# A conditioned residual chain on one core: who issues the first mix weights and the last stores, and the attention table made in four row tiles

## The chip, the cores and the metric

One core of a Trainium2 chip runs the kernel. The metric is the device time of one execution in microseconds (us), the median of several runs.

## The reference

Four residual layers work on x, 32 samples of 128 channels by 2048 positions, all float32. Layers 0 and 3 are grouped convolutions of 9 taps in 4 groups; layers 1 and 2 mix the channels with a matrix that is a softmax-weighted sum of 8 matrices, a different one for every sample.

```python
x = x + conv(x, w0, groups=4, pad=4) + (cond @ c_w0.T)[:, :, None] + side[None, :, None]
for L in (1, 2):
    h   = gelu(gelu(cond @ W0 + b0) @ W1 + b1)
    att = softmax(h @ W2 + b2)                       # 32 x 8
    x   = x + einsum('boi,bih->boh', einsum('bk,koi->boi', att, weight), x) + (att @ bias_k)[:, :, None]
x = x + conv(x, w3, groups=4, pad=4) + (cond @ c_w3.T)[:, :, None] + side[None, :, None]
```

## The kernel before, in words

The positions of a sample are dealt into 4 phases (PH), so that a group of 32 channels times 4 phases fills 128 rows. Every fp32 operand is split into a high and a low part (`x_hi`, `x_lo`, `taps_hi`, ...), and a convolution is 36 turns (TURNS): 12 shifts times three products (high by high, low weights by high, high by low). One turn is four matmuls on four row tiles of 32 rows (`conv_turns`, L836). The two mix layers are one: TensorE multiplies the two matrices of a sample (`product`, L886 and L893), VectorE splits the product into `prod` (`split_product`), four DMAs spread it over the row groups of `mix_w` (`spread_mix_w`, L326), and 48 matmuls apply it (`mix`, L906).

Per sample the order on TensorE is conv0, half of the conv3 of the sample before, product of the next sample, the rest of that conv3, mix. ScalarE makes the high parts (`high_y`, `high_z`, `high_x`), VectorE the low parts (`low_y`, `low_z`, `low_x`) and the sums of 8 matrices (`mix_matrices`, L669, 16 instructions a sample). SyncE issues the loads, the relays, the stores and the spreading of `mix_w`. Engines run in program order and wait on semaphores.

**The start** is written out by hand in each engine's block. TensorE: dummy matmuls (`keep_busy`), the transposes of cond and of the small rows, `hidden(0)`, then the 36 turns of conv0 of sample 0 with the small work put between them: `hidden(1)`, `logits`, the transposes of the context weights, `mix2_transposes(0)`, `contexts`, two transposes of the attention, the matmul that spreads the attention over all rows into the table `att_tab` (L1030), `mix2_transposes(1)`, `conv_biases`, the bias through the mix (`mixed_bias`, 10 matmuls, L955), and after 25 turns `product(zero, 0)`. After turn 36 come 16 turns of conv0 of sample 1, then `mix(zero)`, which waits for `y_lo_done` (the four low parts of y of sample 0, L630) and `mix_w_spread` (the four DMAs, L326, which wait for `prod_lo_done`). VectorE makes the softmax, `att_tab`, the low parts of x, the matrices, the split of the product, 8 more matrix steps, and `low_y(zero)`. ScalarE makes the high taps, the gelus, the exponentials, the planes of sample 1, and then `high_y(zero)` (L465).

**The end.** SyncE's queue stores sample 31 in eight pieces of 128 KB (half h, group g; L378) and between the first four and the last four the two halves of sample 30 (512 KB each, L371), which ScalarE weaves (`weave_half`, L542). The first half's pieces wait for VectorE, the second half's for ScalarE's bias (`bias_last`, L533), which follows VectorE's transposes (L728, L731).

```python
for h in range(2):
    if h == 1:
        for part in range(2):
            sp.wait_ge(halves_woven, part + 1)
            ...
    for g in ((2, 3, 0, 1), range(G))[h]:
        ...
```

Of the kernel before, what the change touches and what calls it, by code (L numbers as in the profile page):

```python
# [24 lines left out]
F32 = mybir.dt.float32  # L25
# [6 lines left out]
G = 4  # L32
# [6 lines left out]
K = 8  # L39
# [7 lines left out]
MIXED = K + 2  # L47
# [3 lines left out]
def conditioned_residual_kernel(nc, x, cond, side, conv0_w, ctx0_w, mix1, mix2, conv3_w, ctx3_w, out):  # L51
# [9 lines left out]
    with ctx:  # L61
# [35 lines left out]
        ones = sb("ones", [GC, C])  # L97
# [17 lines left out]
        key_w = [o1[:, 1544 + K * l:1544 + K * l + K] for l in range(2)]  # L115
        key_b = [o1[0:1, 1560 + K * l:1560 + K * l + K] for l in range(2)]
        bias_k = [o1[0:K, 1576 + 128 * l:1704 + 128 * l] for l in range(2)]
        hid = [[o1[:, 1832 + 32 * (2 * l + m):1864 + 32 * (2 * l + m)] for m in range(2)] for l in range(2)]
# [4 lines left out]
        soft = sb("soft", [N, 64])  # L123
        att_exp = [soft[:, K * l:K * l + K] for l in range(2)]
        att = [soft[:, 16 + K * l:16 + K * l + K] for l in range(2)]
        att_max = [soft[:, 32 + l:33 + l] for l in range(2)]
        att_sum = [soft[:, 34 + l:35 + l] for l in range(2)]
        att_inv = [soft[:, 36 + l:37 + l] for l in range(2)]
        attT_sb = sb("attT_sb", [K, 2, N])
        spread = sb("spread", [N, N, 2 * K])  # L130
# [9 lines left out]
        key_w_in = sem("key_w_in")  # L140
        key_b_in = sem("key_b_in")
# [12 lines left out]
        condT_done = sem("condT_done")  # L154
        ctxT_psum = sem("ctxT_psum")
# [12 lines left out]
        att_step = sem("att_step")  # L168
        spread_done = sem("spread_done")
        attT_psum = sem("attT_psum")  # L170
# [127 lines left out]
        def _(sp):  # L298
# [21 lines left out]
            def spread_mix_w(t, d):  # L320
# [36 lines left out]
            spread_mix_w(zero, 0)  # L357
# [8 lines left out]
            for h in range(2):  # L366
                if h == 1:
                    for part in range(2):
                        sp.wait_ge(halves_woven, part + 1)
                        run = slice(part * L // 2, (part + 1) * L // 2)  # L370
                        sp.dma_start(out[N - 2, :, run].rearrange("(g o) x -> o g x", g=G), out_sb[0][:, run])\  # L371
                          .then_inc(out_stored[0], DMA)
                for g in ((2, 3, 0, 1), range(G))[h]:
                    if h == 0 and g >= 2:
                        sp.wait_ge(last_runs[h], g + 1)
                    else:
                        sp.wait_ge(last_biased[h], g + 1)
                    sp.dma_start(out[N - 1, rows(g), h * L // 2:(h + 1) * L // 2].rearrange("o (i x) -> o i x", i=RUNS),  # L378
                                 last_out[:, h, g, :]).then_inc(out_stored[1], DMA)
# [4 lines left out]
        def _(pool):  # L384
# [48 lines left out]
            for n, m in enumerate((mix1, mix2)):  # L433
                pool.dma_start(key_w[n], m[4]).then_inc(key_w_in, DMA)
                pool.dma_start(key_b[n], m[5].rearrange("(a k) -> a k", a=1)).then_inc(key_b_in, DMA)
            for l, m in enumerate((mix1, mix2)):
                pool.dma_start(bias_k[l], m[7]).then_inc(bias_k_in, DMA)
# [7 lines left out]
        def _(act):  # L445
# [45 lines left out]

            def gelus(m):
                act.wait_ge(hidden_psum, m + 1)
                for l in range(2):
                    act.activation(hid[l][m], ps[:, 6, 64 + 32 * (2 * m + l):96 + 32 * (2 * m + l)], ACT.Gelu,
                                   bias=mlp_b[l][m]).then_inc(hidden_done, 1)
# [47 lines left out]

            def product_out(t, d):
# [547 lines left out]
```

## Time and profile before

| | us |
|---|---|
| median of 3 runs | 663.0 (662.95 to 663.0) |
| the profiled execution's own time | 663.23 |
| its span, first to last instruction | 661.4 |
| TensorE busy | 650.6 |
| last matmul ends | 652.84 |
| `mix(zero)` starts | 31.29 |

The profile covers one execution, with times from the start of its span. A timeline row gives start, duration, engine, line, operation, output and inputs, and in brackets how long the engine was idle before it and what ended that. SPq and ACTq are DMA issues in the instruction streams of SyncE and ScalarE. The chain of waits is the work that ended last, followed back from the end. A matmul row of "x2" can be one fp32 matmul, which shows as two passes.

### The profile page before, as it was taken

How to read it: one execution, taken by the hardware profiler on the slowest of the kernel's cores; microseconds unless marked ns; L12 is line 12 of the kernel's file. 1: busy time of each engine (PE TensorE's matmuls, PEld its weight loads, DVE VectorE, ACT ScalarE, POOL GpSimd, SP SyncE). 2: the span in 40 equal slices, each digit the busy share in tenths (PEclk: the TensorE clock that was granted, in tenths of full speed). 3: DMA queues.
4: the chain of work that ended last, by engine and by line, in shares of the span. 5: the costliest groups of instructions: out<-in, count | busy, mean ns of one | idle time of the engine just before them, and what ended most of it. 6: DMA issues, size and time to landing. Idle time of an engine off the chain costs nothing.

```text
span 661.4 us, 24661 instructions
## 1 busy us (share of the span) xinstructions
PE 650.6 (98%) x11220; PEld 595.9 (90%) x11220; DVE 476.5 (72%) x945; ACT 262.3 (40%) x328; POOL 241.7 (37%) x85
## 2 busy tenths in 40 slices
PE   8999999999999999999999999999999999999994
PEld 6889999999999999999999999999999999999994
DVE  7898867687767677677677677677677677677635
ACT  4643424433424433424433423433423433433434
POOL 3024334433424433434443433442433442433220
PEclk9999999999999999999999999999999999999998
DMA  7355776454566455566455566545566545444515
GB/s 235 97 162 161 224 224 213 155 175 183 168 222 219 153 168 191 159 222 222 156 163 194 154 222 222 165 153 199 150 223 223 164 154 205 153 154 161 159 67 192
DMA packets 50325, 118.77 MB, mean 180 GB/s; under 512 B 5557, under 2 KB 26090, under 8 KB 42474
## 3 DMA queue, kind: packets, MB, share of 16 engines
q1 hardware_dynamic: 49602, 117.48, 54.7%
q8 instruction: 28, 0.46, 0.3%
q10 hardware_dynamic: 488, 0.69, 0.3%
q14 instruction: 15, 0.12, 0.1%
q0 software_dynamic: 192, 0.02, 0.0%
HBM read 35.33 MB, written 33.55 MB: 104 GB/s over the span
## 4 chain that ended last, share of the span: by engine, by line
PE 96%; DVE 1%; DMA 1%; SPq 0%; ACTq 0%; ACT 0%; issue 0%
PE ps L836 79%; PE ps L906 14%; PE ps L893 1%; DMA out_planes<-in_L_cond_b 1%; PE ps L874 1%; DVE x_in L728 1%; DMA mix_w<-prod 1%; DVE x_planes L731 0%; PE ps L955 0%; SPq L326 0%; PE ps L943 0%; ACTq L554 0%; ACT x_planes L533 0%; PE ps L981 0%; PE ps L886 0%
## 5 line engine op out<-in xcount | busy, mean ns | idle before, releaser
L399 POOL COPY out_sb<-out_planes 128x2048 f32<-128x2048 f32 x30 | 118.7, 3956 | 220.4 <-DVE mat2T L669 208.4
L390 POOL COPY x_planes<-x_in 128x2048 f32<-128x2048 f32 x29 | 112.7, 3887 | 137.8 <-DVE x_lo L616 137.8
L465 ACT ACTIVATE y_hi<-ps,bias_tab 128x512 fp32r<-128x512 f32 x128 | 77.5, 689 | 189.1 <-PE ps L836 189.1
L640 DVE SCALAR_TENSOR_TENSOR z_lo<-ps,bias_tab,z_hi 128x1024 fp32r<-128x1024 f32 x62 | 76.8, 1280 | 69.2 <-ACT z_hi L475 69.2
L630 DVE SCALAR_TENSOR_TENSOR y_lo<-ps,bias_tab,y_hi 128x512 fp32r<-128x512 f32 x128 | 87.3, 745 | 38.9 <-ACT y_hi L465 38.9
L836 PE MATMUL ps<-z_hi,taps_lo 32*128 32x512 f32 x1488 | 99.4, 397 | 0.0
L836 PE MATMUL ps<-x_hi,taps_hi 32*128 32x512 f32 x1536 | 97.2, 391 | 0.0
L836 PE MATMUL ps<-x_hi,taps_lo 32*128 32x512 f32 x1536 | 96.5, 389 | 0.0
L836 PE MATMUL ps<-x_lo,taps_hi 32*128 32x512 f32 x1536 | 96.0, 390 | 0.0
L836 PE MATMUL ps<-z_hi,taps_hi 32*128 32x512 f32 x1488 | 92.9, 391 | 0.0
L483 ACT ACTIVATE out_taps<-ps,bias_tab 128x512 f32<-128x512 f32 x62 | 39.3, 684 | 134.3 <-PE ps L836 134.3
L836 PE MATMUL ps<-z_lo,taps_hi 32*128 32x512 f32 x1488 | 92.5, 390 | 0.0
L906 PE MATMUL ps<-y_hi,mix_w 32*128 32x512 f32 x1024 | 89.8, 389 | 0.3 <-DMA mix_w<-prod 0.3
L836 PEld LDWEIGHTS ps<-x_hi,taps_hi 32*128 32x128 f32 x1536 | 82.4, 184 | 7.1 <-issue 0.4
L836 PEld LDWEIGHTS ps<-x_lo,taps_hi 32*128 32x128 f32 x1536 | 82.2, 183 | 7.1
L836 PEld LDWEIGHTS ps<-x_hi,taps_lo 32*128 32x128 f32 x1536 | 82.4, 183 | 6.7 <-issue 0.2
L836 PEld LDWEIGHTS ps<-z_hi,taps_hi 32*128 32x128 f32 x1488 | 79.9, 183 | 7.0
L836 PEld LDWEIGHTS ps<-z_lo,taps_hi 32*128 32x128 f32 x1488 | 80.0, 183 | 6.7
L475 ACT ACTIVATE z_hi<-ps,bias_tab 128x1024 fp32r<-128x1024 f32 x62 | 65.7, 1112 | 50.0 <-PE ps L906 50.0
L836 PEld LDWEIGHTS ps<-z_hi,taps_lo 32*128 32x128 f32 x1488 | 77.0, 184 | 5.7
L616 DVE TENSOR_TENSOR x_lo<-x_planes,x_hi 128x2048 fp32r<-128x2048 f32 x31 | 70.8, 2284 | 0.0
L650 DVE TENSOR_SCALAR out_taps<-ps,bias_tab 128x512 f32<-128x512 f32 x62 | 43.7, 747 | 23.2 <-PE ps L836 23.2
(122 smaller groups left out, 554.2 us busy)
## 6 DMA issues: line engine op xcount, KB each, us to landing
x_in<-in_x SPq DMA_DIRECT2D x31, 1024.0 KB, 5.2
out_planes<-out_taps SPq DMA_DIRECT2D x122, 256.0 KB, 2.5
out<-out_sb SPq DMA_DIRECT2D x30, 1024.0 KB, 4.5
mix_w<-prod SPq DMA_DIRECT2D x128, 128.0 KB, 3.6
x_in<-in_x SPq DMA_DIRECT2D x2, 512.0 KB, 5.4
out<-x_planes SPq DMA_DIRECT2D x8, 128.0 KB, 2.1
out<-out_sb SPq DMA_DIRECT2D x2, 512.0 KB, 3.5
out_taps<-in_L_cond_weight SPq DMA_DIRECT2D x1, 512.0 KB, 6.5
```

The lines of the kernel that those rows point to most:

```text
L390: pool.tensor_copy(x_planes[:, :, :], planes(x_in[t.par(d)], slice(0, S))).then_inc(x_planed, 1)
L399: pool.tensor_copy(out_sb[t.par(d)][:, :].rearrange("c (s p) -> c p s", p=PH), out_planes[:, :, :])\
L465: act.activation(y_hi[:, g, :], ps[:, bank(t, 0) + g, :], ACT.Identity, bias=bias_tab[:, b, g:g + 1]).then_inc(y_hi_done, 1)
L475: act.activation(z_home(t, 0)[0][:, 2 * h:2 * h + 2, 1:S + 1], ps[:, k:k + 2, :], ACT.Identity, bias=bias_tab[:, b, 2 * G:BIAS]).then_inc( ...
L483: act.activation(out_taps[:, g, :], ps[:, bank(t, d) + g, :], ACT.Identity, bias=bias_tab[:, b, G + g:G + g + 1]).then_inc(out_act, 1)
L616: dve.tensor_tensor(out=x_lo[p][:, :, 1:S + 1], in0=x_planes[:, :, :], in1=x_hi[p][:, :, 1:S + 1].bitcast(F32), op=ALU.subtract).then_inc( ...
L630: dve.scalar_tensor_tensor(out=y_lo[:, g, :], in0=ps[:, bank(t, 0) + g, :], scalar=bias_tab[:, b, g:g + 1], in1=y_hi[:, g, :].bitcast(F32) ...
L640: dve.scalar_tensor_tensor(out=z_home(t, 0)[1][:, 2 * h:2 * h + 2, 1:S + 1], in0=ps[:, k:k + 2, :], scalar=bias_tab[:, b, 2 * G:BIAS], in1 ...
L650: dve.tensor_scalar(out_taps[:, g, :], ps[:, bank(t, d) + g, :], bias_tab[:, b, G + g:G + g + 1], None, ALU.add).then_inc(out_dve, 1)
L728: dve.transpose(blocks(last_mid[:, h, g, :]), taps).then_inc(last_turned[h], 1)
L836: tile = pe.matmul(ps[:, first_bank + g, :], w[rows(g), d, :], a[rows(g), d % PH, d // PH:d // PH + S], start=(n == 0), stop=(n == TURNS - 1))
L906: tile = pe.matmul(ps[:, bank(t, 0) + p, :], w[rows(p), g, h, :], a[rows(p), g, :], start=(n == 0), stop=(n == 3 * G - 1))
```

## The change

- **End**: the first half of sample 30 is stored by SyncE after two of the eight pieces of sample 31; the second half is issued by ScalarE (`store_woven`), between its weave and `bias_last`. SyncE issues nine stores instead of ten.
- **First mix weights**: of the four DMAs that spread `mix_w` of sample 0, SyncE issues two and ScalarE two (`spread_first`), ahead of `high_y(zero)`. One of ScalarE's four `taps_high(1, p)` moves behind `high_y(zero)`.
- **Attention**: `hid` of the second layer is stored four times side by side (128 columns), so the logits come out on 128 rows, the same 32 samples in each of four row groups; both softmaxes run as one set of instructions; each row group keeps its own 8 samples (`own_samples`), and four matmuls of 32 rows by 128 columns, on four row tiles, make the table instead of one of 32 rows by 512. The transposed attention comes from a VectorE transpose of 32x32, and both layers' keys for the bias are one operand of 16 rows, so `mixed_bias` has 9 matmuls instead of 10.
- **Order of the start**: `hidden(0)` stands ahead of the wait for the small rows; `contexts` and `conv_biases` move back; `product(zero, 0)` comes after 34 turns instead of 25; 18 turns of conv0 of sample 1 stand ahead of `mix(zero)` instead of 16. On VectorE the low parts of x come in single phases and mostly behind the table; on ScalarE both `plane_x1` come behind `agg`.

The diff, cut:

```diff
-MIXED = K + 2
+MIXED = K + 1
+SAMPLES = N // G
...
             zero = Step(0, 0)
-            spread_mix_w(zero, 0)
+            spread_mix_w(zero, 0, range(2))
...
             relay_out(ALL[N], -2, range(2))
-            for h in range(2):
-                if h == 1:
-                    for part in range(2):
-                        sp.wait_ge(halves_woven, part + 1)
...
+            store_group(0, 2)
+            store_group(0, 3)
+            sp.wait_ge(halves_woven, 1)
+            sp.dma_start(out[N - 2, :, 0:L // 2].rearrange("(g o) x -> o g x", g=G), out_sb[0][:, 0:L // 2])\
+              .then_inc(out_stored[0], DMA)
+            store_group(0, 0)
+            store_group(0, 1)
+            for g in range(G):
+                store_group(1, g)
...
+            def spread_first():
+                act.wait_ge(prod_hi_done, 1)
+                act.wait_ge(prod_lo_done, 1)
+                for p in range(2, PH):
+                    act.dma_start(mix_w[0][rows(p), :, :, :].rearrange("o g h z -> o g (h z)").bitcast(F32),
+                                  prod[:, :, :].rearrange("m h z -> m (h z)").bitcast(F32))\
+                       .then_inc(mix_w_spread[0], DMA)
...
+            def store_woven():
+                act.wait_ge(halves_woven, 2)
+                act.dma_start(out[N - 2, :, L // 2:L].rearrange("(g o) x -> o g x", g=G), out_sb[0][:, L // 2:L])\
+                   .then_inc(out_stored[0], DMA)
...
-            for p in range(PH):
+            for p in range(PH - 1):
                 taps_high(1, p)
...
             act.wait_ge(bias_tab_done, 3)
+            spread_first()
             high_y(zero)
+            taps_high(1, PH - 1)
             high_z(zero)
...
             weave_half(1)
+            store_woven()
             bias_last()
...
+            def spread_attention():
+                pe.wait_ge(spread_done, 1)
+                pe.wait_ge(mix2T_done, 1)
+                for r in range(G):
+                    pe.matmul(ps[:, G + r, 384:512], ones[rows(r), :], spread[rows(r), :, :].rearrange("n m k -> n (m k)"),
+                              start=True, stop=True).then_inc(att_tab_psum, 1)
...
-            conv0(zero, range(14, 19))
+            conv0(zero, range(19, 25))
             for k in range(MIXED // 2):
                 mixed_bias(k)
-            conv0(zero, range(19, 25))
+            conv0(zero, range(25, 31))
             for k in range(MIXED // 2, MIXED):
                 mixed_bias(k)
+            conv0(zero, range(31, 34))
             product(zero, 0)
-            conv0(zero, range(25, TURNS))
+            conv0(zero, range(34, TURNS))
 
             pe.wait_ge(bias_tab_done, 3)
             pe.wait_ge(prod_summed, 1)
-            conv0(first, range(16))
+            conv0(first, range(18))
             mix(zero)
-            conv0(first, range(16, TURNS - 4))
+            conv0(first, range(18, TURNS - 4))
```

TensorE's order between the last part of `mixed_bias` and `mix(zero)`, before and then now (lines of conv0, product and mix are L836, L886, L906 before and L887, L937, L957 now):

```order
L955 MATMUL ps<-attT_sb,out_sb 128x32 x2
L886 MATMUL ps<-mat2T,mat 128x128 [waits mats_step]
L836 MATMUL ps<-x_lo,taps_hi 128x512 x44
L836 MATMUL ps<-x_hi,taps_hi 128x512 [waits x_hi_done,prod_summed,bias_tab_done]
L836 MATMUL ps<-x_hi,taps_hi 128x512 x47
L836 MATMUL ps<-x_hi,taps_lo 128x512 x16
L906 MATMUL ps<-y_hi,mix_w 128x512 [waits mix_w_spread0,y_lo_done]
```

```order
L1008 MATMUL ps<-attT_sb,out_sb 128x32
L887 MATMUL ps<-x_lo,taps_hi 128x512 x12
L937 MATMUL ps<-mat2T,mat 128x128 [waits mats_step]
L887 MATMUL ps<-x_lo,taps_hi 128x512 x8
L887 MATMUL ps<-x_hi,taps_hi 128x512 [waits x_hi_done,prod_summed,bias_tab_done]
L887 MATMUL ps<-x_hi,taps_hi 128x512 x47
L887 MATMUL ps<-x_hi,taps_lo 128x512 x24
L957 MATMUL ps<-y_hi,mix_w 128x512 [waits mix_w_spread0,y_lo_done]
```

Between the product and the mix that uses it stood 27 turns (108 matmuls) and stand 20 now (80 matmuls).

ScalarE's order around the first high part of y, before and now:

```order
L489 ACTIVATE taps_hi<-taps_raw 128x288 [waits taps_raw_step1,taps_zeroed1] x4
L598 ACTIVATE bias_tab<-ps 128x32 [waits mixed_psum]
L465 ACTIVATE y_hi<-ps,bias_tab 128x512 [waits conv0_done,bias_tab_done]
L465 ACTIVATE y_hi<-ps,bias_tab 128x512 [waits conv0_done] x3
L475 ACTIVATE z_hi<-ps,bias_tab 128x2x512 [waits mix_done,bias_tab_done]
```

```order
L506 ACTIVATE taps_hi<-taps_raw 128x288 [waits taps_raw_step1,taps_zeroed1] x3
L633 ACTIVATE bias_tab<-ps 128x32 [waits mixed_psum]
L514 DMA mix_w<-prod 32x4x256 [waits prod_lo_done,prod_hi_done,bias_tab_done]
L514 DMA mix_w<-prod 32x4x256
L482 ACTIVATE y_hi<-ps,bias_tab 128x512 [waits conv0_done] x4
L506 ACTIVATE taps_hi<-taps_raw 128x288 [waits taps_raw_step1,taps_zeroed1]
```

Two DMA issues and a wait for the split product now stand between the bias table and `y_hi`.

SyncE's order at the end, before and now (L371 and L391 store halves of sample 30, L378 and L384 pieces of sample 31):

```order
L313 DMA out_planes<-out_taps 128x1x512 x2
L378 DMA out<-x_planes 32x4x256 x4
L371 DMA out<-out_sb 32x4x1024 x2
L378 DMA out<-x_planes 32x4x256 x4
```

```order
L325 DMA out_planes<-out_taps 128x1x512 x2
L384 DMA out<-x_planes 32x4x256 x2
L391 DMA out<-out_sb 32x4x1024
L384 DMA out<-x_planes 32x4x256 x6
```

One half went to ScalarE, the other is now third instead of fifth.

## Rows read from the trace of the kernel before

**Rows 1.** Busy time by stretches: length, then busy us and instructions of each engine.

```profile
48.05:640.00 591.95, 591.95 (x10301) 546.77 (x10299) 423.70 (x824) 226.78 (x269) 231.40 (x59) 1.00 0.56 182
...
652.84:661.40 8.56, 0.00 (x0) 0.00 (x0) 3.97 (x9) 3.39 (x5) 0.00 (x0) 0.73 0.67 245
```

**Rows 2.** The chain of waits, start: start, us, what.

```profile
14.64 0.12 PE ps L1025
...
15.10 0.47 PE ps L1030
...
15.80 0.29 PE ps L1030
...
18.44 1.38 PE ps L836 x14
...
22.65 1.34 PE ps L955 x10
23.99 0.43 PE ps L886 x2
```

**Rows 3.** The chain of waits: 54 turns of convolution without a stop.

```profile
624.70 12.57 PE ps L836 x216
```

**Rows 4.** The timeline, 5 to 32 us.

```profile
5.80 0.69 DVE L689 STREAM_TRANSPOSE taps_raw<-out_sb 128x288 f32<-128x288 f32 x1 [1.64 <-DMA out_sb<-in_L_cond_weight]
...
6.71 2.09 DVE L771 CAST x_hi<-x_in 128x1024 fp32r<-128x1024 f32 x2
...
9.11 1.22 PE L836 MATMUL ps<-x_hi,taps_hi 32*128 32x512 f32 x16
...
18.67 2.07 ACT L455 ACTIVATE x_planes<-x_in 128x1024 f32<-128x1024 f32 x1
...
25.03 0.29 DVE L682 TENSOR_TENSOR prod<-prod_sum,prod 128x128 fp32r<-128x128 f32 x1
...
25.41 2.87 SPq L326 DMA_DIRECT2D mix_w<-prod  x4
...
27.08 0.34 DVE L669 SCALAR_TENSOR_TENSOR mat2T<-mix_wT,att_tab,acc 128x128 f32<-128x128 f32 x1
27.25 2.42 ACT L465 ACTIVATE y_hi<-ps,bias_tab 128x512 fp32r<-128x512 f32 x4 [2.15 <-PE ps L836]
28.04 2.73 DVE L630 SCALAR_TENSOR_TENSOR y_lo<-ps,bias_tab,y_hi 128x512 fp32r<-128x512 f32 x4 [0.61 <-ACT y_hi L465]
...
31.29 0.51 PE L906 MATMUL ps<-y_hi,mix_w 32*128 32x512 f32 x4 [0.31 <-DMA mix_w<-prod]
```

**Rows 5.** Line L326 (the DMAs that spread `prod`), the first 40 us: issue to landing.

```profile
DMA to landing us min/median/max: 3.3/3.5/3.6
```

**Rows 6.** The timeline, the end.

```profile
645.90 1.45 ACTq L521 DMA_DIRECT2D out_planes<-out_taps  x2
...
650.38 3.93 ACT L542 ACTIVATE out_sb<-out_planes 128x1024 f32<-128x1024 f32 x2 [0.91 <-DMA out_planes<-out_taps]
...
654.52 0.96 ACT L533 ACTIVATE x_planes<-x_planes,bias_tab 128x256 f32<-128x256 f32 x2 [0.22 <-DVE x_planes L731]
654.74 1.25 SPq L371 DMA_DIRECT2D out<-out_sb  x2
...
656.39 0.96 ACT L533 ACTIVATE x_planes<-x_planes,bias_tab 128x256 f32<-128x256 f32 x2 [0.91 <-DVE x_planes L731]
```

**Rows 7.** The timeline of SyncE's issues in short stretches, stores of sample 31.

```profile
656.86 1.21 SPq L378 DMA_DIRECT2D out<-x_planes  x1
...
658.76 0.60 SPq L378 DMA_DIRECT2D out<-x_planes  x1
```

**Rows 8.** Line L378: issue to landing.

```profile
DMA to landing us min/median/max: 2.1/2.1/3.5
```

**Rows 9.** Busy time by stretches, the stores; the last two columns are DMA share, GB/s.

```profile
653.20:655.90 2.70, 0.00 (x0) 0.00 (x0) 2.70 (x7) 2.07 (x3) 0.00 (x0) 1.00 0.58 194
655.90:660.30 4.40, 0.00 (x0) 0.00 (x0) 0.91 (x3) 0.96 (x2) 0.00 (x0) 0.60 0.92 348
```

More of the change, by code:

```diff
@@ L365, in _, with store_group @@
             relay_out(ALL[N], -2, range(2))
-            for h in range(2):
-                if h == 1:
-                    for part in range(2):
-                        sp.wait_ge(halves_woven, part + 1)
[L370 to L379, printed above, removed]
+            def store_group(h, g):
+                if h == 0 and g >= 2:
+                    sp.wait_ge(last_runs[h], g + 1)
+                else:
+                    sp.wait_ge(last_biased[h], g + 1)
+                sp.dma_start(out[N - 1, rows(g), h * L // 2:(h + 1) * L // 2].rearrange("o (i x) -> o i x", i=RUNS),
+                             last_out[:, h, g, :]).then_inc(out_stored[1], DMA)
+            store_group(0, 2)
[7 more added lines that the diff above has]
+                store_group(1, g)
             sp.wait_ge(out_stored[0], DMA * (N // 2 + 1))
@@ L586, in _ @@
             act.activation(agg[:, :], ps[:, 6, 320:320 + N], ACT.Copy).then_inc(agg_done, 1)
+            plane_x1(0)
             plane_x1(1)
@@ new lines, in _ @@
+            dve.wait_ge(att_tab_psum, G)
+            dve.tensor_copy(att_tab[:, :, :].rearrange("c (r m) k -> c r (m k)", r=G),
+                            ps[:, G:2 * G, 384:512]).then_inc(att_tab_done, 1)
+            for p in range(1, PH):
+                low_direct(0, half(0), slice(p, p + 1))
+                low_direct(0, half(1), slice(p, p + 1), p == PH - 1)
+                if p == 1:
+                    dve.wait_ge(ctx_psum, 1)
+                    dve.wait_ge(mlp_cols_done, 1)
+                    dve.wait_ge(of_group_done, 1)
+                    ctx_columns(0)
+                    ctx_columns(1)
@@ L1019, in _ @@
             last.then_inc(ctxT_psum, 2)
-            conv0(zero, range(7, 10))
+            conv0(zero, range(6, 10))
             mix2_transposes(0)
-            contexts()
-            pe.wait_ge(att_step, 4)
-            for l in range(2):
-                last = pe.transpose(ps[0:K, 6, 256 + N * l:256 + N * l + N], att[l], ident[0:N, 0:N])
-            last.then_inc(attT_psum, 1)
             conv0(zero, range(10, 11))
-            pe.wait_ge(spread_done, 1)
-            pe.wait_ge(mix2T_done, 1)
-            pe.matmul(ps[:, 4, :], ones[0:N, :], spread[:, :, :].rearrange("n m k -> n (m k)"), start=True, stop=True)\
-              .then_inc(att_tab_psum, 1)
+            spread_attention()
             conv0(zero, range(11, SHIFTS))
             pe.wait_ge(taps_lo_done[0], PH)
-            conv0(zero, range(SHIFTS, 14))
+            conv0(zero, range(SHIFTS, 15))
+            contexts()
             mix2_transposes(1)
```

141 lines of the change are left out of this document (78 added, 63 removed).

## The prediction

> **What bounds the kernel now.** I read the table of stretches first: between 48 and 640 us TensorE is busy for all of 591.95 us [rows 1]. The change touches nothing there, so it can gain or lose only in the two stretches around it: the start, in which the small work of the conditioning is fitted between convolution turns, and the 8.56 us after the last matmul, in which TensorE does nothing [rows 1]. In the start TensorE's work is all needed, so time is lost only where it waits, where it does something that can be made smaller, or where a change between full-height and row-tiled matmuls drains it. What a turn costs is in the undisturbed chain: 216 matmuls in 12.57 us, 54 turns, 0.233 us a turn [rows 3]. Five turns after full-height work took 1.38 us instead of 1.16 [rows 2], so each interruption of the turns costs about 0.2 us beside its own work.
>
> The chain of waits shows two more places. `mix(zero)` started at 31.29 behind the mix weights' DMA, after only 0.31 us of idle time [rows 4]: there the cover and the DMAs were almost even. At the end, ScalarE's last bias ran from 656.39 to 657.35 [rows 6], but SyncE issued the last store only at 658.76 [rows 7]; it landed 2.1 us later [rows 8], 0.5 us before the span ended. So the last store was 1.4 us late to its data, because SyncE's stream was behind.
>
> **The end.** Before, SyncE issued ten stores, at 0.60 us and a short gap each (two in 1.25 us [rows 6]), one of them longer, 1.21 us from 656.86 [rows 7]. Now nine: counting on from 652.16 in steps of 0.65 us, the two pieces, the half of sample 30 at 653.45 (its weave, half of ScalarE's 3.93 us from 650.38 [rows 6], is done at 652.45), two pieces, then the four of the second half from 655.4, each behind its bias. ScalarE issues the other half at about 654.35. Two ACT issues took 1.45 us [rows 6], so one is 0.72: the first pair of biases moves from 654.52 to about 655.05. The second pair stays, since it waits for VectorE until 656.39 [rows 6]. The third and fourth pieces are then bound by the biases: the last is issued at about 657.4 instead of 658.76. **Bound on the good side: 1.35 us gained.**
>
> The other end is the bytes. From 653.2 to 655.9 the pieces move at 194 GB/s, because 128 KB are issued every 0.65 us; after that the halves are in flight and it is 348 GB/s at a DMA share of 0.92 [rows 9]. Now the first half is in the stream 1.3 us sooner, so for 1.3 us the engines move 348 GB/s instead of 194: 0.20 MB less remain, worth 0.58 us at 348. If the engines' share is what held the last pieces, **0.6 us** is the gain. The before was not at that bound at its very end (the last piece landed in the shortest time of all, 2.1 us), so the truth is between; I take **1.0 us**, the middle of the two.
>
> The Trainium skill, page DMA: Bandwidth & Descriptors, section Issuing engines are not separate DMA queues, says that DMAs issued from several engines share the same 16 DMA engines and that only the sequencer's issue time is saved. By it the second queue would be worth the issue it takes off SyncE, about 0.65 us by the rows above, and the sum would end 0.35 us later.
>
> **The start, until the product.** Steps on TensorE, as changes of the time at which `product(zero, 0)` ends (24.42 before [rows 2]):
> - `hidden(0)` no longer stands behind the small rows. Convolution then starts when VectorE's cast of sample 0 ends, 6.71 + 2.09 = 8.80 [rows 4], so at about 8.87 instead of 9.11: **-0.24**. The eight-column and 32-column copies and fills added on VectorE fall into its 1.64 us wait for the taps' load [rows 4] and cost nothing; were that wait gone, up to six instructions of 0.2 us, 1.2 us in all, would push the cast.
> - The logits use 128 columns of weights and six passes instead of eight of 32; a pass with 128 columns took 0.134 (ten in 1.34 [rows 2]). 0.80 against 0.62: **+0.15**.
> - The attention: the two transposes (0.12) and the spreading matmul (0.47 and 0.29) go [rows 2], and four row tiles of 128 columns, two passes each, come. By their columns they are a quarter of 0.76, with the drain 0.35. The softmax ends a microsecond sooner, but the table's matmuls now wait for ScalarE's copy of the first transposes out of the same bank, about 0.25 us. Sum **-0.3**.
> - `mixed_bias` loses one matmul, two passes of 0.134 [rows 2]: **-0.26**.
> - `conv_biases` and the product each stand alone now: two more interruptions, **+0.4**.
> - Nine more turns ahead of the product: 2.1 us later on the clock, but no time, since they are taken from behind it.
>
> So the product ends at 24.42 - 0.25 + 2.1 = about 26.3. VectorE's sixteen matrix steps take 0.26 us each (eight between 25.32 and 27.42 [rows 4]) and end at 24.6 by my count, so it is not they that set it. ScalarE has both `plane_x1` behind `agg` now, 2.07 us more ahead of the bias table [rows 4], less one `taps_high`, and gives the bias table at about 26.5, just ahead of TensorE's need at 26.8: no cost, with 0.3 us to spare.
>
> **The start, from the product to the mix.** This is where the change adds a wait. Write P for the end of the product. Before, P was 24.42, `prod` complete at 25.32, VectorE's eight further matrix steps done at 27.42, `y_hi` began at 27.25, `y_lo` at 28.04 and ended at 30.77, the DMAs were issued from 25.41 on [rows 4] and landed at most 3.6 us after their issue [rows 5]. Now:
> - cover: 20 turns, 4.66 us, to P + 4.9 with the drain;
> - weights: two issues side by side on two streams, the second at P + 1.75, landed at P + 5.2;
> - `y_lo`: ScalarE waits for the product's split (P + 0.9), issues two DMAs (1.45 [rows 6]), and only then begins `y_hi`; `y_lo` follows 0.79 later and takes 2.73 [rows 4]: P + 5.9. VectorE alone, with its eight steps first, would give P + 3.0 + 2.73 = P + 5.7, nearly the same.
>
> So the mix waits for `y_lo`, not for the DMA: P + 5.9 = 32.2, 0.9 us later than 31.29. Two more turns (0.47 us) are done by then. The start is **0.45 us worse** on balance, less what I may have over-counted in the drains; I enter **+0.3**. Bounds: if `y_lo` does not hold (ScalarE's issues are off its path and the matrix steps slip behind), the mix starts at TensorE's own pace and the start gains 0.25 + 0.3 = 0.55; if the lateness is carried on (VectorE's low parts of z, the next split and the next spreading of weights all come about 0.9 us later, and the mix of sample 1 stands 0.1 to 0.5 us behind its DMAs), it loses 0.9.
>
> **Sum.** 663.0 + 0.3 - 1.0 = **662.3 us**. The profiled execution took 663.23 with a span of 661.4; against it the forecast is a span of 660.7. The median of the runs lies 0.2 us below that execution.
>
> **Rivals.** A measurement of this kernel can tell about 0.2%, 1.3 us, from no change.
> - *The mix is not late.* The start gains 0.55 and the end 1.0 to 1.35: 661.1 to 661.45, faster. For it: the change shortens the very DMAs for which the chain waited. Against it: the program order on ScalarE, and the cover cut from 27 to 20 turns. It needs `y_lo` done by P + 4.9, a microsecond sooner than its steps add up. Chance 0.2.
> - *The bytes hold the end.* Second half on its own stream or not, the last piece lands when the engines are through: gain 0.3 to 0.6, and with the start's +0.3 this is 662.7 to 663.0. The page's rule points this way. For it: share 0.92 [rows 9], and the one long issue of 1.21 us [rows 7]. Against it: the last piece took the shortest time of all. Chance 0.2.
> - *The wait travels.* Slower than before: the product's late split delays `y_lo`, then `z_lo`, then the second split, and `mix_w` of sample 1 lands after TensorE asks for it. At 0.9 us in the start and 0.6 at the end this is 663.3; it is slower by over 1.3 us only if the mix of sample 0 starts 1.9 us late or more, that is past 33.7, which needs DMAs from ScalarE's stream that land later than 5.5 us after their issue. Nothing in the rows shows that. Chance 0.1 for the mechanism, 0.05 for the time over 664.3.
> - *My forecast's own case*, mix late by 0.7 to 1.1, end 0.8 to 1.35 sooner: 661.9 to 662.8. Chance 0.5.
>
> **How the numbers follow.** The forecast's own case gives 662.3. The range takes in the bytes' case and the mild form of the travelling wait, up to 663.5, and downwards most of the case in which the mix is not late, down to 661.3; below it and above it some 2 in 10 are left. Faster by over 0.2% (below 661.7) needs the first rival or the very best end: 0.22. Slower (above 664.3): 0.05. The rest, 0.73, is within 0.2%.
>
> **What would show it.** Right: convolution of sample 0 begins near 8.9; the product ends near 26.3; the row at the first matmul of `mix` names VectorE's `y_lo` as its releaser with an idle time of about 1 us, and it starts near 32.2; ScalarE has two DMA issues between the split and `y_hi`; TensorE's last matmul ends 0.3 us later than before, and the last store is issued near 657.7; from the last matmul to the end 7.6 us instead of 8.56. Wrong: a first mix behind a DMA or without idle time, an issue of over a microsecond among SyncE's last four, or an idle TensorE between 40 and 60 us.

## The result and the profile after

The changed kernel took 664.47 us in the median of 20 executions (663.76 to 666.19), the kernel before 663.15 in 20 on the same chip: a ratio of 1.0025 on record, interval 1.0019 to 1.0031 (the ratio of the means is 1.0024, of the medians 1.0020). It is slower by 1.3 us; the forecast was 662.3, with a range up to 663.5. The times fall into two groups: 14 from 663.76 to 664.76, median 664.34, and six from 665.82 to 666.19. The profiled execution, 665.82 with a span of 664.0, is one of the six. The table splits the loss; the terms are worked out below.

| | us against before |
|---|---|
| start, up to the first mix | +1.54 |
| the mix itself, in 6 of 20 executions | +1.55 |
| after the last matmul | -0.52 |
| sum in the profiled execution | +2.57 (spans: 664.0 - 661.4 = 2.6) |

The chain of waits of the changed kernel, start; columns as in [rows 2]. It answers to the last row of [rows 2] and the last of [rows 4]:

```profile
2.58 1.18 DVE own_samples L807
...
26.12 0.43 PE ps L937 x2
...
27.55 0.70 SPq L338
28.30 4.86 DMA mix_w<-prod
...
33.30 4.62 PE ps L957 x47
37.92 3.30 PE ps L887 x56
41.22 0.42 PE ps L937 x2
41.64 6.49 PE ps L887 x92
```

`product(zero, 0)` ends at 26.55 instead of 24.42, 2.13 us later, but the DMAs behind it (L338, L514) are still the releaser of the first `mix` (L957). They land at 28.30 + 4.86 = 33.16. TensorE was through with its 20 turns at 33.30 - 1.87 = 31.43. Behind the mix, TensorE goes on without a wait: the next product and the 92 matmuls after it are end to end.

The timeline of the changed kernel in the same stretch, for [rows 4]:

```profile
2.52 1.84 DVE L807 COPY own_samples<-ident 32x8 f32<-32x8 f32 x4
...
3.64 0.10 POOL L449 MEMSET z_lo<- 128x8 f32 x1
...
7.06 2.08 DVE L815 CAST x_hi<-x_in 128x1024 fp32r<-128x1024 f32 x2
...
9.28 0.97 PE L887 MATMUL ps<-x_hi,taps_hi 32*128 32x512 f32 x12 [0.45 <-DVE x_hi L815]
...
27.55 1.64 SPq L338 DMA_DIRECT2D mix_w<-prod  x2
27.57 1.61 ACTq L514 DMA_DIRECT2D mix_w<-prod  x2
...
29.23 2.42 ACT L482 ACTIVATE y_hi<-ps,bias_tab 128x512 fp32r<-128x512 f32 x4 [2.98 <-issue]
...
30.02 2.73 DVE L668 SCALAR_TENSOR_TENSOR y_lo<-ps,bias_tab,y_hi 128x512 fp32r<-128x512 f32 x4 [0.46 <-ACT y_hi L482]
...
33.30 0.79 PE L957 MATMUL ps<-y_hi,mix_w 32*128 32x512 f32 x4 [1.87 <-DMA mix_w<-prod]
```

The wait ahead of the mix is 1.87 us instead of 0.31, and the mix starts 33.30 - 31.29 = 2.01 us later, with two more turns (0.47) done by then: 1.54 lost. `y_lo` ended at 32.75, 0.4 us ahead of the DMAs.

The two lines that issue the four DMAs, from issue to landing, L338 (SyncE) and then L514 (ScalarE), for [rows 5]:

```profile
DMA to landing us min/median/max: 3.3/4.1/4.9
...
DMA to landing us min/median/max: 4.2/4.3/4.3
```

Four issues in turn landed at 3.3 to 3.6 us each, the last 31.16 - 25.41 = 5.75 us after the first issue [rows 4]. Issued two by two they take up to 4.9 each, and the last lands 33.16 - 27.55 = 5.61 us after the first issue. The two streams bought 0.14 us, though all four were issued within 1.64 us instead of 2.87.

Busy time by stretches, over the mix; the last three columns are granted clock, DMA share and GB/s:

```profile
33.30:36.50 3.20, 3.20 (x32) 3.01 (x36) 3.20 (x8) 0.00 (x0) 0.00 (x0) 0.51 0.61 192
36.50:37.90 1.40, 1.40 (x28) 1.37 (x24) 0.54 (x3) 0.00 (x0) 0.00 (x0) 0.91 0.84 339
```

From the mix's first matmul on, after TensorE had been idle for 1.87 us, the granted clock is 0.51 for 3.2 us: the lower of the two levels, 1.2 GHz. The mix took 4.62 us for 47 matmuls, and 3.07 in the kernel before. The two groups of times are 1.62 us apart (medians 665.96 and 664.34), so this is nearly all of their distance.

The timeline at the end, for [rows 6, 7]:

```profile
655.31 1.24 SPq L384 DMA_DIRECT2D out<-x_planes  x2
...
656.59 0.60 SPq L391 DMA_DIRECT2D out<-out_sb  x1
...
657.65 0.63 ACTq L578 DMA_DIRECT2D out<-out_sb  x1
...
658.86 1.09 SPq L384 DMA_DIRECT2D out<-x_planes  x1
...
659.54 0.96 ACT L563 ACTIVATE x_planes<-x_planes,bias_tab 128x256 f32<-128x256 f32 x2 [0.31 <-DVE x_planes L769]
...
661.43 0.61 SPq L384 DMA_DIRECT2D out<-x_planes  x1
```

and by stretches, for [rows 9]:

```profile
657.70:659.00 1.30, 0.00 (x0) 0.00 (x0) 1.30 (x4) 0.67 (x2) 0.00 (x0) 0.61 0.92 365
659.00:663.40 4.40, 0.00 (x0) 0.00 (x0) 0.96 (x3) 1.20 (x3) 0.00 (x0) 0.50 0.86 309
```

The last matmul ends at 655.96, 8.04 us ahead of the end instead of 8.56. The last bias ends at 660.50, and the last store is issued 0.93 us later, where 1.4 us were before. One of SyncE's issues still takes 1.09 us, and the DMA engines reach a share of 0.92 by 657.70, 1.74 us after the last matmul; before, the stretch at 0.92 began 3.06 us after it.

### The profile page after: what moved, and what is told of

Read it like the earlier page. It is cut to its first block, busy times and chain, and to the rows that moved or that the text cites. A ratio compares the mean times of both kernels' runs of the same rounds, so it can differ in the third digit from the quotient of the medians.

```text
span 664.0 us, 24675 instructions
## 1 busy us (share of the span) xinstructions
PE 652.0 (98%) x11219; PEld 554.6 (84%) x11219; DVE 477.9 (72%) x954; ACT 262.5 (40%) x328; POOL 241.7 (36%) x85
## 4 chain that ended last, share of the span: by engine, by line
PE 96%; DVE 2%; DMA 1%; ACT 0%; issue 0%; POOL 0%; SPq 0%; POOLq 0%; ACTq 0%; DVEq 0%
PE ps L887 79%; PE ps L957 14%; PE ps L944 1%; DMA mix_w<-prod 1%; PE ps L925 1%; DVE x_in L766 1%; DVE x_planes L769 0%; PE ps L1008 0%; DVE own_samples L807 0%; DVE x_hi L815 0%; PE ps L996 0%; ACT x_planes L563 0%; PE ps L937 0%; DVE taps_raw L727 0%; SPq L338 0%
## 5 line engine op out<-in xcount | busy, mean ns | idle before, releaser
L887 PE MATMUL ps<-z_hi,taps_lo 32*128 32x512 f32 x1488 | 98.9, 397 | 0.0
L887 PE MATMUL ps<-x_hi,taps_hi 32*128 32x512 f32 x1536 | 95.9, 391 | 0.4 <-DVE x_hi L815 0.4
L887 PE MATMUL ps<-x_lo,taps_hi 32*128 32x512 f32 x1536 | 96.3, 391 | 0.0
L887 PE MATMUL ps<-x_hi,taps_lo 32*128 32x512 f32 x1536 | 95.7, 389 | 0.0
L887 PE MATMUL ps<-z_hi,taps_hi 32*128 32x512 f32 x1488 | 92.4, 391 | 0.0
L887 PE MATMUL ps<-z_lo,taps_hi 32*128 32x512 f32 x1488 | 92.0, 390 | 0.0
L957 PE MATMUL ps<-y_hi,mix_w 32*128 32x512 f32 x1024 | 88.5, 394 | 1.9 <-DMA mix_w<-prod 1.9
L887 PEld LDWEIGHTS ps<-x_hi,taps_hi 32*128 32x128 f32 x1536 | 76.3, 184 | 13.8 <-ACT taps_hi L506 0.9
L887 PEld LDWEIGHTS ps<-x_lo,taps_hi 32*128 32x128 f32 x1536 | 76.4, 183 | 12.9
L887 PEld LDWEIGHTS ps<-x_hi,taps_lo 32*128 32x128 f32 x1536 | 76.5, 183 | 12.2
L887 PEld LDWEIGHTS ps<-z_hi,taps_hi 32*128 32x128 f32 x1488 | 73.7, 183 | 13.3
L887 PEld LDWEIGHTS ps<-z_lo,taps_hi 32*128 32x128 f32 x1488 | 73.8, 183 | 12.9
L887 PEld LDWEIGHTS ps<-z_hi,taps_lo 32*128 32x128 f32 x1488 | 71.3, 184 | 11.0
L957 PEld LDWEIGHTS ps<-y_hi,mix_w 32*128 32x128 f32 x1024 | 51.7, 185 | 11.3 <-DVE y_lo L668 2.3
```

What stands on the lines that cost most here:

```text
L887: tile = pe.matmul(ps[:, first_bank + g, :], w[rows(g), d, :], a[rows(g), d % PH, d // PH:d // PH + S], start=(n == 0), stop=(n == TURNS - 1))
L957: tile = pe.matmul(ps[:, bank(t, 0) + p, :], w[rows(p), g, h, :], a[rows(p), g, :], start=(n == 0), stop=(n == 3 * G - 1))
```

## The experiments

**Theories.** For the start: the four spreading DMAs take about the same time however they are issued, so a product that ends later with less work behind it is a longer wait (the main theory); rivals are ScalarE's detour over two issues (which delays `y_hi` and `y_lo`) and the small copies that VectorE now makes ahead of the cast. For the two groups of times: TensorE's clock falls after a long enough wait, or something else in the start disturbs it. For the end: the bytes, or SyncE's stream. The batches were run on three chips; the kernel before stood at 663.15, 663.22 and 663.21 in them.

**1. The new end alone**, in the kernel before.

```diff
             weave_half(1)
+            store_woven()
             bias_last()
```

and SyncE's nine stores in the new order.

> The kernel before with the new order of the last stores alone. Theory A (the end gains half a microsecond, all the loss is in the start): 0.5 us faster than before, about 662.6, and from the last matmul to the end 8.0 us instead of 8.56. Rival B (the end gains nothing, its 8.0 us in the changed kernel came from a chance state of the DMAs): 663.1, within 0.1 us of before. Rival C (the end is worth the full microsecond of the prediction once the start is undisturbed): 662.1.

Measured: 662.81 (662.49 to 662.98), ratio 0.9992 (0.9983 to 1.0001): 0.34 us sooner in the median, which the interval does not tell from none. The row of SyncE's pieces of sample 31 (L371 here), with the min/median/max ns of an issue:

```profile
L371 SPq DMA_DIRECT2D out<-x_planes x8: 590/608/1170, 652.2 to 658.3; - x8
```

The long issue is still there, 1.17 us, and the last issue comes at 658.35 instead of 658.76, 0.9 us behind the last bias (657.43). By these two, and by the 0.52 of the changed kernel's profile, the end gains a third to a half of the 1.0 that was entered; the medians alone would not show it.

**2. The new start alone**: the changed kernel with the old end.

```diff
             weave_half(1)
-            store_woven()
             bias_last()
```

> The changed kernel with the old order of the last stores. Theory A: 0.5 us slower than the changed kernel, about 665.0 in the median, with an idle time of about 1.9 us ahead of the first mix and a lower granted clock behind it in some executions. Rival B: the same as the changed kernel, 664.5.

Measured in five executions, median 666.50: 664.54, 664.67, 666.5, 666.57, 666.67; ratio 1.0044 (1.003 to 1.0057). Both groups are there again, so both come from the start. The profiled execution was 664.54; its timeline:

```profile
27.53 1.82 ACTq L510 DMA_DIRECT2D mix_w<-prod  x2
...
29.40 2.42 ACT L478 ACTIVATE y_hi<-ps,bias_tab 128x512 fp32r<-128x512 f32 x4 [3.20 <-issue]
...
33.04 0.51 PE L952 MATMUL ps<-y_hi,mix_w 32*128 32x512 f32 x4 [1.59 <-DVE y_lo L663]
```

Here the two issues held ScalarE for 1.82 us, `y_hi` began at 29.40, and `y_lo` (done at 32.93) is named as the releaser, as the forecast had it. So `y_lo` and the DMAs come within some tenths of each other, and either can be last. The mix took 3.08 us in this execution, at full clock.

**3. All four spreading DMAs back on SyncE**, the rest as changed.

```diff
-            spread_mix_w(zero, 0, range(2))
+            spread_mix_w(zero, 0)
...
-            spread_first()
             high_y(zero)
```

> The changed kernel with all four DMAs of the first mix weights issued by SyncE again. Theory A (the four DMAs of 128 KB are held by the DMA engines, not by their issue, so two streams gain nothing): the last of them lands 5.6 to 5.8 us after the first issue as before, the mix still waits 1.8 to 2.0 us, y_lo ends about 0.5 us sooner, and the time is that of the changed kernel within 0.3 us. Rival D (two streams do save their issue time, 1.2 us here): the mix comes a microsecond or more later, 665.5 or above.

Measured: 664.99 (seven executions, four from 664.31 to 664.99, three from 666.12 to 666.24), ratio 1.0029 (1.0018 to 1.004): no gain. The timeline of the profiled execution:

```profile
27.57 3.16 SPq L338 DMA_DIRECT2D mix_w<-prod  x4
...
33.60 0.51 PE L956 MATMUL ps<-y_hi,mix_w 32*128 32x512 f32 x4 [2.17 <-DMA mix_w<-prod]
```

With ScalarE's detour gone, `y_hi` began at 27.31 and `y_lo` was done at 32.21, 1.4 us ahead of the mix. The mix still waited, for the DMAs, which landed at 33.46, 5.89 us after the first issue. The detour is therefore not what costs; it only ties with the DMAs.

This profile is of the upper group, and the clock fell here too, 0.45 us into the mix, which took 4.61 us:

```profile
33.60:38.20 4.60, 4.60 (x52) 4.32 (x56) 2.91 (x9) 0.00 (x0) 0.00 (x0) 0.63 0.93 338
```

**4. The 32x8 copies moved back on VectorE**, behind the cast of sample 0.

```diff
-            for r in range(G):
-                ...
             for w in (taps_hi[1], taps_lo[1]):
...
+            for r in range(G):
+                ...
             dve.wait_ge(logits_psum, 1)
```

> The changed kernel with the four copies into own_samples moved behind the first low parts of x. Theory A (the first copy lasted 1.18 us because it ran beside GpSimd's fills, and it pushed the cast of x and the convolution's start by 0.35 us): the copies take 0.2 us each there, the cast ends near 8.8, convolution starts near 8.9, and the kernel is 0.35 us faster than the changed one, about 664.1. Rival E (the start of convolution does not matter, since the mix waits for the weights, whose product hangs on other engines): no difference, 664.5.

Measured: 664.12 (ten executions from 663.69 to 664.31, one of 666.07), ratio 1.0014 (1.0005 to 1.0023). The two rows of the copies, ns min/median/max, of the changed kernel and then of this one:

```profile
L807 DVE COPY own_samples<-ident x4: 161/170/1246, 2.5 to 4.2; 32x8 f32<-32x8 f32 x4
```

```profile
L822 DVE COPY own_samples<-ident x4: 148/160/168, 11.3 to 11.8; 32x8 f32<-32x8 f32 x4
...
33.26:36.30 3.04, 3.04 (x52) 2.92 (x56) 3.04 (x7) 0.00 (x0) 0.00 (x0) 1.00 0.63 202
```

In the changed kernel the first copy lasted 1.25 us and ended at 3.76, just as GpSimd's last fill did (3.64 + 0.10). The Trainium skill, page SBUF — State Buffer, section Who interferes with whom, says that a copy on VectorE can take the port pair it shares with GpSimd, and that whichever comes first holds it for its whole instruction. The trace agrees that the copy is held, but not by one instruction: GpSimd's fills last 0.41 us at most, and the copy stood behind the whole row of them. Moved, no copy takes over 0.17, VectorE has its wait for the taps' load back (1.63 us), convolution starts at 9.02 instead of 9.28 and the product ends at 26.26. The median falls by 0.35; the ten lower executions have a median of 663.96, 0.38 below the changed kernel's lower group. The profiled execution does not show this gain at the mix, which starts at 33.26: its DMAs took 5.88 us from the first issue. The last row is the stretch of the mix: it waited 2.08 us here, and the clock stayed at 1.00. So such a wait does not always bring the fall. (One upper execution of 11 against 6 of 20 is too few to say that it became rarer.)

**5. The product three turns sooner** (after 31 turns, the wait's cover 23 turns).

```diff
-            conv0(zero, range(31, 34))
             product(zero, 0)
-            conv0(zero, range(34, TURNS))
+            conv0(zero, range(31, TURNS))
```

> The changed kernel with the product of sample 0 after 31 turns instead of 34, directly behind the last part of mixed_bias. Theory A (the loss is the interval from the product to the mix, 6.6 us of split and DMAs behind 20 turns of cover): the product ends 0.8 to 0.9 us sooner, the wait ahead of the first mix falls from 1.9 to about 1.0 us, no lower clock behind it in any execution, and the median is 0.9 to 1.1 us below the changed kernel, about 663.5. Rival F (the attention in four row tiles and the two more interruptions cost the time, the wait only shows it): at most 0.2 us faster, for the one interruption less.

Measured: 663.72 (663.29 to 664.04), ratio 1.0005 (0.9996 to 1.0014). First mix:

```profile
33.03 0.50 PE L957 MATMUL ps<-y_hi,mix_w 32*128 32x512 f32 x4 [1.32 <-DMA mix_w<-prod]
```

Three turns are 0.70 us, but the product ends only 0.37 sooner, at 26.18: VectorE's matrices are not ready before. The wait falls to 1.32 and the group above 665 is gone.

**6. Four more turns ahead of the mix** (22 instead of 18).

```diff
-            conv0(first, range(18))
+            conv0(first, range(22))
```

> The changed kernel with 22 turns of the next convolution ahead of the first mix instead of 18; all other work is the same. Theory A: the wait ahead of the mix falls by 0.93 us to about 0.95, the mix starts at the same time (33.2), nothing later waits for z_lo, and the median is 0.9 us lower, about 663.6, without executions near 666. Rival G (the wait only moves: with 10 turns instead of 14 behind the mix, the product of sample 1 or the convolution after it waits for z_lo): 664.2 to 664.5.

Measured: 663.76 (663.19 to 664.16), ratio 1.0008 (0.9999 to 1.0017). Two rows of the timeline:

```profile
32.79 0.50 PE L957 MATMUL ps<-y_hi,mix_w 32*128 32x512 f32 x4 [0.39 <-DMA mix_w<-prod]
...
38.53 0.46 PE L937 MATMUL ps<-mat2T,mat 128*128 128x128 f32 x2 [0.35 <-DVE z_lo L678]
```

The wait ahead of the mix is covered but for 0.39, and part of it comes back at the next product, 0.35 us behind `z_lo`, which follows the mix: fewer turns are left between them. Again no execution above 665.

**7. All repairs together**: 3, 4, 5 and 6, with the new end.

> The changed kernel with four repairs: the four copies late, the product after 31 turns, 22 turns ahead of the first mix, all four weight DMAs on SyncE; the new end is kept. Theory A: product ends near 25.4, weights land near 32.0, TensorE reaches the mix near 31.8, a wait of 0.2 to 0.5 us; faster than both kernels, 662.3 (0.85 us below before). Rival G (the wait moves behind the mix, to z_lo): 662.8 to 663.2.

Measured: 662.79 (662.62 to 663.26), ratio 0.9994 (0.9985 to 1.0003). That is experiment 1's 662.81: even so repaired, the new start gives nothing over the old one. Its waits are shorter, not gone: the product ended at 25.30, the DMAs landed at 32.20 (first issue 26.30), the mix waited 0.57, and the next product another 0.35 behind `z_lo`. What the new start would be worth without these two is not shown.

**8. Only the two streams**, in the kernel before: `spread_first` with two of the four DMAs on ScalarE.

```diff
-            spread_mix_w(zero, 0)
+            spread_mix_w(zero, 0, range(2))
...
+            spread_first()
             high_y(zero)
```

> The kernel before with one part of the change alone: two of the four first weight DMAs issued by ScalarE ahead of high_y. Theory A (the four transfers are held by the DMA engines): the last lands 5.6 to 5.8 us after the first issue as before, but y_hi begins 0.2 us or more later, y_lo ends near 31.0, and the time is within 0.2 us of before. Rival D (the issue is what holds them): the last lands a microsecond sooner and the wait of 0.31 us ahead of the mix goes: 662.8.

Measured: 663.02 (662.69 to 663.70), ratio 0.9997 (0.9988 to 1.0006). The timeline:

```profile
25.34 1.64 SPq L326 DMA_DIRECT2D mix_w<-prod  x2
25.36 1.61 ACTq L497 DMA_DIRECT2D mix_w<-prod  x2
...
31.10 0.51 PE L916 MATMUL ps<-y_hi,mix_w 32*128 32x512 f32 x4 [0.19 <-DMA mix_w<-prod]
```

The last lands at 30.96, 5.62 us after the first issue, where one stream took 5.75 [rows 4]. The Trainium skill, page DMA: Bandwidth & Descriptors, section Issuing engines are not separate DMA queues, says that several issuing engines share the same 16 DMA engines and save only sequencer time. This agrees: the four issues were out 1.23 us sooner after the first (1.64 us instead of 2.87), the last landing 0.13 us.

SyncE's next issue, the 1 MB load of a later sample, also comes sooner now (27.02 instead of 28.32) and could have eaten the gain. The trace's DMA packets speak against it: the spreading's 1 KB packets run from 26.69 to 29.91 (26.77 to 30.07 before), and the load's first packet starts at 29.32 (29.58 before), so it meets only their last 0.6 us (0.5 before).

**9. The end without the second half of sample 30**, otherwise as experiment 1: this kernel leaves that half of the output out.

```diff
             weave_half(1)
-            store_woven()
             bias_last()
```

> The kernel before with the new order of the last stores, and the second half of sample 30 not stored at all (it leaves that half of the output out). Theory H (at the end the bytes in flight hold SyncE's issues and landings): with 0.5 MB less the last store is issued right behind its bias and the kernel is 0.8 to 1.0 us faster than e1, about 661.9. Rival I (SyncE's own pace of 0.65 us a store holds the end): no faster than e1, 662.8.

Measured: 661.93 (661.63 to 662.39), ratio 0.9982 (0.9973 to 0.9991), 0.88 less than experiment 1. SyncE's pieces:

```profile
L371 SPq DMA_DIRECT2D out<-x_planes x8: 545/601/790, 652.2 to 657.5; - x8
```

No long issue (0.79 at most), and the last at 657.51, 0.16 us behind the last bias (657.35). The edit also takes an issue off ScalarE, but that moved the last bias by only 0.08 us (657.43 in experiment 1), and SyncE's order is the same in both. So the 512 KB, not the order of SyncE's stream, lengthen an issue and keep the last store late.

**10. The kernel before, with the new end and 18 turns instead of 16 ahead of the mix.**

```diff
-            conv0(first, range(16))
+            conv0(first, range(18))
             mix(zero)
```

> The kernel before with the new order of the last stores and 18 instead of 16 turns ahead of the first mix, everything else of the start as before. Theory A (the start's loss came from what the change did to the product and its cover, and the wait of 0.3 us ahead of the mix can be filled): mix starts at 31.45, two more turns are done, 0.3 us faster than e1: 662.5. Rival G (the later product and convolution wait for z_lo instead): the same as e1, 662.8.

Measured: 662.38 (661.94 to 662.64), ratio 0.9988 (0.9979 to 0.9996). The chain of waits:

```profile
23.71 0.42 PE ps L897 x2
24.13 7.05 PE ps L847 x103
31.18 2.80 PE ps L917 x48
```

From the product to the end of the mix TensorE never waits. It is faster than both kernels: 0.8 us below the one before (the interval only just excludes 1) and 2.1 below the changed one. Against experiment 1 it gained 0.43, which is the old wait of 0.31 and a little more. (In its profiled execution the whole start ran 0.3 us ahead, which has nothing to do with the turns.)

**11. Four turns fewer ahead of the mix** (14 instead of 18), the rest as changed: a longer wait, to see whether the clock follows.

```diff
-            conv0(first, range(18))
+            conv0(first, range(14))
```

> The changed kernel with 14 instead of 18 turns ahead of the first mix; all work is the same. It lengthens TensorE's wait from 1.9 to 2.8 us. Theory J (the executions near 666 are those in which the granted clock falls after the wait, and a longer wait makes that the rule): nearly all executions have the lower clock behind the wait, the mix takes 4 us or more instead of 3.07, median 664.4 + 0.9 + 1.5 = 666.8. Rival K (the falls have another cause): two levels as before, most executions near 665.3.

Measured in six executions, median 666.68: 665.12, 665.28, 666.62, 666.74, 668.09, 668.16; ratio 1.0053 (1.0038 to 1.0068). Four of six are above the lowest pair, in two steps of 1.5 us, so the fall is now the more common case, and in two executions its cost is doubled (their mean granted clock is 0.991, against 0.993 in the two at 666.6 and 666.7). First mix of the profiled execution (666.62) and the stretches behind it:

```profile
33.20 0.51 PE L957 MATMUL ps<-y_hi,mix_w 32*128 32x512 f32 x4 [2.64 <-DVE y_lo L668]
```

```profile
34.00:35.00 1.00, 1.00 (x20) 0.79 (x16) 1.00 (x1) 0.00 (x0) 0.00 (x0) 0.69 0.34 139
35.00:36.00 1.00, 1.00 (x16) 0.84 (x12) 1.00 (x4) 0.00 (x0) 0.00 (x0) 0.50 0.00 0
36.00:37.00 1.00, 1.00 (x16) 0.84 (x12) 1.00 (x5) 0.00 (x0) 0.00 (x0) 0.50 0.61 106
37.00:38.00 1.00, 1.00 (x16) 0.81 (x15) 0.44 (x2) 0.16 (x1) 0.00 (x0) 0.60 0.90 352
```

The granted clock falls to 0.50 after a wait of 2.64 us, this time about 1.2 us into the mix, and is back some 3 us later; the mix took 4.54 us.

**12. Half the bytes**: experiment 8 with only the high part of each row spread, 64 KB a DMA instead of 128.

```diff
-                    sp.dma_start(mix_w[0][rows(p), :, :, :], prod[:, :, :])
+                    sp.dma_start(mix_w[0][rows(p), :, 0, :], prod[:, 0, :])
```

(bitcasts and reshaping left out here; ScalarE's two alike. The low half of `mix_w`, which is not spread now, is filled with zeros by GpSimd, and the issues wait for that fill too: the first comes at 25.58 instead of 25.34.)

> The kernel e8 (two streams of weight DMAs in the kernel before) with only the high parts of the first product spread, 64 KB a DMA instead of 128 KB (the low parts of the first mix weights are zeros, so sample 0's mix is computed with high parts alone). Theory A (the engines' work on the bytes holds the four DMAs): the last lands about 1.4 us sooner after the first issue, 4.2 instead of 5.6 us, the wait ahead of the mix is gone, mix at 30.9. Rival L (the number of pieces, which is the same, holds them): 5.6 us as before and the wait of 0.2 us stays.

Measured: 662.75 (662.42 to 663.13), ratio 0.9993 (0.9985 to 1.0002). The two lines' landing times:

```profile
DMA to landing us min/median/max: 2.4/2.7/3.0
...
DMA to landing us min/median/max: 2.7/2.8/2.9
```

The second pair was issued at 26.3, so the last landed by 29.3, 3.7 us after the first issue instead of 5.62. Half the bytes in the same number of pieces save 1.9 us, two streams 0.13: the bytes hold these transfers. The DMA packets in the two traces split the interval. From the first issue to the first packet it is 1.35 us in both; the packets take 3.2 us in experiment 8 and 1.6 here, so 0.8 us for each 128 KB; and from the last packet to the landing it is 1.05 and 0.75 us. With one stream the issues went out at nearly the same pace as the bytes, 2.87 us for four or 0.72 each. So two limits of about the same length stood side by side, and taking away the issues alone brought next to nothing.

## Why the prediction was wrong

- **Convolution starts at 8.87: wrong by 0.4.** It started at 9.28. The step that said that the small copies "fall into its 1.64 us wait for the taps' load and cost nothing" missed that the first of them lasts 1.25 us beside GpSimd's fills. The taps' data were there in time and the wait was gone, the case that the step itself named and set aside. Experiment 4 puts 0.35 us of the median on it.
- **The product ends at 26.3: about right.** It was 26.55, and 26.26 with the copies moved. From the first turn to the product's end the steps gave 17.4 us and the trace shows 17.3. The cover was right too: P + 4.9, measured P + 4.88.
- **"Weights: two issues side by side on two streams, the second at P + 1.75, landed at P + 5.2": this is the step that failed.** They landed at P + 6.6. I took a DMA's landing time (up to 3.6 us) as belonging to each issue by itself, so that issuing sooner would mean landing sooner; issued two by two they took up to 4.9. Experiments 3, 8 and 12 show the bytes of the four together to be the limit: 5.6 to 5.9 us from the first issue, on one stream or two. The sum should have kept the old 5.75 us and put it at the new place. That gives a landing at 27.55 + 5.75 = 33.3, where 33.16 was measured. With it the releaser was wrong as well: the mix waited 1.87 us for the DMA, and not about 1 us for `y_lo`, in the profiled execution.
- **`y_lo` at P + 5.9: nearly right.** It was P + 6.2, because ScalarE's two issues took 1.61 and VectorE was ready. In experiments 2 and 11 it was even named as the releaser. Experiment 3 shows that its removal alone gains nothing.
- **The start is 0.3 worse: it was 1.54 worse.** 1.1 of it is the mix at 33.30 instead of 32.2, and 0.15 what I had taken off for over-counting.
- **TensorE's clock: not in the forecast at all.** [Rows 1] show a granted clock of 1.00 in the long stretch and I did not ask what a longer wait does to it. In 6 of 20 executions the mix ran at about half clock and took 1.55 us more. That is 0.1 us of the median and about 0.5 of the mean. The inference that the upper group of times is this fall rests on the profiles: the three that were taken of an execution above the lowest group show it (the changed kernel, experiments 3 and 11: a mix of 4.62, 4.61 and 4.54 us), and two of the lowest group do not (experiments 2 and 4: 3.08 and 3.07 at full clock). It rests further on the mean granted clock (0.993 to 0.994 in the six executions, 0.996 to 0.998 in the fourteen), and on experiments 5 to 7 and 11, in which the group goes and comes with the wait.
- **The end gains 1.0: it gained 0.34 (experiment 1) to 0.52 (this profile).** I had taken the middle between the issues (1.35) and the bytes (0.6); the bytes' rival was right and even its 0.6 was the upper edge. The row that I held against it, the last piece's landing in the shortest time, does not speak against the bytes: the waiting can be done before, in a lengthened issue. Experiment 9 settles it.
- **The rivals.** "The bytes hold the end" came true. "The mix is not late" fell. "The wait travels" came near in its price, and not by its mechanism. Nothing was passed on, as the 92 matmuls behind the next product show. Its condition was not met either: 663.0 plus a net loss of 1.9 in the start less 0.6 at the end needs a mix past 33.7, which is 2.4 us late and not 1.9, since two more turns are done by then. The mix started at 33.30, a net loss of 1.54, and no DMA took 5.5 us from its own issue (4.9 at most here, 5.1 in experiment 4). That the median still passed 664.3 comes from the smaller gain at the end and from the upper group. The interval that mattered stood in [rows 4]: 5.75 us from first issue to last landing, with the product 2.1 us later.
- **The sum.** From 662.3 to 664.47 it is 2.17 us: 1.24 in the start, 0.66 at the end (by experiment 1), 0.13 by the clock, and 0.15 because the kernel before stood at 663.15 and not at 663.0.

What stays open: why a wait of 2.08 us left the clock alone in one execution while 1.87 brought it down in another, and how long a wait it takes; the runs give shares only. Also open is what lengthens an issue in the spreading (below).

## What to carry to other kernels

Ask of several equal DMAs how long they take together, from the first issue to the last landing, and let that interval travel as a whole when their producer moves; more issuing engines shorten it only if issuing was the limit. When work is moved from behind a producer to ahead of it, the cover shrinks at once and by all of it, so count both the new time of the producer and the turns that are left. And a wait of TensorE near 2 us is to be priced with what it can do to the clock, not with its length alone.

## What was unexpected of the hardware

- A wait of 1.6 to 2.6 us of TensorE in the middle of full work is followed, in a part of the executions, by about 3 us at half clock. Sorted by the wait in the profiled execution of each kernel: with 1.3 us or less (experiments 5, 6, 7) none of 33 executions shows it, with 1.6 to 2.2 (the changed kernel, experiments 2, 3, 4) 13 of 43, with 2.6 (experiment 11) 4 of 6. It costs 1.5 us, in two cases of experiment 11 twice that.
- Four 128 KB DMAs within SBUF need 5.6 to 5.9 us from first issue to last landing, half the bytes 3.7. Some 2.4 of the 5.6 us are not bytes: 1.35 ahead of the first packet and 1.05 behind the last.
- At the end of the kernel an issue of a DMA takes 1.1 to 1.2 us instead of 0.60 while the DMA engines are at a share of 0.92; with 512 KB less none is over 0.79 (experiment 9). In the spreading the second issue takes 0.59 to 1.12 us on one stream and 0.85 to 1.35 with two. There the cause is not shown: the first DMA's packets have not or only just begun by then (share 0.00 from 28.05 to 28.55 and 0.22 up to 29.05 in the changed kernel), and with half the bytes it still takes 1.0 us (experiment 12). Either way the issuing engine is held for that time, so an engine with computing to do pays for it: ScalarE's second issue of 1.10 us in experiment 2 made `y_hi` later.
- A copy of 32x8 elements on VectorE can last 1.25 us instead of 0.16 beside a row of GpSimd's fills, none of them over 0.41. Fills on VectorE in the same place (experiment 4) kept their 0.38 us.
